# Distance attention: the clamp and the copy of the row minima on VectorE, exponentials over two key tiles

## The reference

```python
q2 = jnp.sum(q * q, axis=-1)
k2 = jnp.sum(k * k, axis=-1)
qk = jnp.einsum('bhid,bhjd->bhij', q, k)
d2 = jnp.maximum(q2[..., :, None] + k2[..., None, :] - 2.0 * qk, 1e-12)
attn = jax.nn.softmax(-jnp.sqrt(d2), axis=-1)
out = jnp.einsum('bhij,bhjd->bhid', attn, v)
...
x = x + (out @ wo.T + bo) * g
```

## Time and profile before

| what | value |
|---|---|
| median of 3 runs | 3808.49 us |
| the profiled execution: its own time | 3799.39 us |
| its span | 3797.3 us |
| mean granted TensorE clock over the span | 0.907 |
| the distance stage in it, from the first minimum to the end | about 3099 to 3797 us |
| mean length of a group's step, from 3432 to 3684 us (12 steps) | 21.0 us |
| busy in these 252 us: ACT, POOL, DVE, PE | 240.5, 231.0, 217.5, 196.0 us |

### The profile page before, as it was taken

How to read it: one execution, slowest core, us unless ns; L and a number is a source line. 1 busy time by engine, 2 the same in 40 slices (tenths; PEclk the granted TensorE clock), 3 DMA queues, 4 the chain that set the end, 5 groups by cost and what they waited for, 6 DMA issues and landing times. The chain is left out here.

```text
span 3797.3 us, 55242 instructions
## 1 busy us (share of the span) xinstructions
PE 3184.6 (84%) x16225; PEld 1672.8 (44%) x16225; DVE 3031.4 (80%) x4845; ACT 2297.1 (60%) x2738; POOL 1814.5 (48%) x904
## 2 busy tenths in 40 slices
PE   7767888888997997877889999899987777877776
PEld 3322333332335886655523334499975531111111
DVE  6878999999995776865678988577757768888887
ACT  4776666667772334643446666522226549999998
POOL 0008998999993111011200000034436538999996
PEclk9878999999998998987879999999998877888888
DMA  4543333323322345955742334144444733344432
GB/s 127 200 175 121 144 146 145 145 96 145 124 69 74 110 152 162 207 139 187 248 136 73 77 72 95 48 101 89 88 78 159 204 105 105 115 127 120 129 117 84
DMA packets 313743, 478.18 MB, mean 126 GB/s; under 512 B 50839, under 2 KB 256280, under 8 KB 293134
## 3 DMA queue, kind: packets, MB, share of 16 engines
q1 hardware_dynamic: 256894, 408.82, 33.8%
q10 hardware_dynamic: 44432, 51.10, 5.0%
q0 software_dynamic: 12288, 16.79, 2.7%
HBM read 322.48 MB, written 153.91 MB: 125 GB/s over the span
## 5 line engine op out<-in xcount | busy, mean ns | idle before, releaser
L1225 PE MATMUL mamba_psum<-mamba_hc,scan_ident 128*128 128x512 f32 x1024 | 548.7, 643 | 90.1 <-DVE mamba_hc L1133 72.1
L3643 POOL TENSOR_TENSOR distance_dist<-distance_dist,distance_least_all 128x2048 f32<-128x2048 f32 x124 | 559.0, 4540 | 74.9 <-DMA distance_least_all<-distance_least_rows 74.8
L1156 DVE TENSOR_TENSOR_SCAN mamba_psum<-mamba_psum,mamba_drive 128x512 f32<-128x512 f32 x352 | 414.9, 1216 | 22.9 <-issue 10.5
L2784 DVE TENSOR_REDUCE causal_row_max<-causal_psum 128x1 f32<-128x512 f32 x512 | 333.0, 683 | 78.0 <-PE causal_psum L2854 68.0
L1225 PEld LDWEIGHTS mamba_psum<-mamba_hc,scan_ident 128*128 128x128 f32 x1024 | 175.8, 195 | 418.0 <-DVE mamba_hc L1133 254.9
L2743 ACT ACTIVATE causal_probs<-causal_psum 128x1024 f32<-128x1024 f32 x256 | 250.6, 1021 | 122.0 <-PE causal_psum L2877 121.8
L3819 PE MATMUL distance_psum<-distance_shared_k_stacks,distance_shared_q_stacks 102*128 102x512 bf16 x512 | 208.7, 504 | 116.9 <-DVE distance_least L3737 56.5
L3737 DVE TENSOR_REDUCE distance_least<-distance_psum 128x2 f32<-128x1024 f32 x256 | 294.2, 1213 | 8.3 <-PE distance_psum L3819 8.0
L3773 DVE TENSOR_SCALAR distance_dist<-distance_psum 128x1024 f32<-128x1024 f32 x192 | 227.0, 1219 | 80.5 <-PE distance_psum L3834 80.5
L1076 POOL TENSOR_TENSOR mamba_drive<-late_channels,scan_b_all 128x1024 f32<-128x1024 f32 x64 | 149.9, 2355 | 289.3 <-POOLq L32 289.3
L1120 ACT ACTIVATE mamba_psum<-mamba_dt,scan_a_neg 128x512 f32<-128x512 f32 x256 | 167.3, 683 | 140.8 <-DVE mamba_hc L1133 140.3
(11 more groups left out here) (473 smaller groups left out, 8593.3 us busy)
## 6 DMA issues: line engine op xcount, KB each, us to landing
distance_least_all<-distance_least_rows SPq DMA_DIRECT2D x32, 1024.0 KB, 4.7
scan_b_all<-bc SPq DMA_DIRECT2D x16, 1024.0 KB, 4.6
scan_c_all<-bc SPq DMA_DIRECT2D x16, 1024.0 KB, 6.6
mamba_b_all<-bc SPq DMA_DIRECT2D x16, 1024.0 KB, 5.1
mamba_c_all<-bc SPq DMA_DIRECT2D x16, 1024.0 KB, 7.1
choice_w<-L_ffn_w SPq DMA_DIRECT2D x16, 1024.0 KB, 5.4
z<-mamba_in_z SPq DMA_DIRECT2D x8, 1024.0 KB, 3.9
xc<-mamba_in_xc SPq DMA_DIRECT2D x8, 1024.0 KB, 3.9
```

The source lines that it names most:

```text
L1156: dve.tensor_tensor_scan(out, bank, drive[:, n % DRIVES], 0.0, ALU.mult, ALU.add).then_inc(h_ready, 1)
L1225: pe.matmul(ps[:, Y_BANK + m % 2], ident[:, :], hc[:, n % PRODUCTS], start=False, stop=(s == DS - 1)).then_inc(y_summed, 1)
L2784: dve.reduce_max(row_max[:, g % 2, u:u + 1], ps[:, u % 2], AX.X).then_inc(a_max, 1)
L3643: pool.tensor_tensor(dist[:, g % 2, kt], dist[:, g % 2, kt], least_all[:, g % 2], ALU.subtract).then_inc(shifted, 1)
```

## The change

```diff
@@ -3558,6 +3558,7 @@
         UNITS = GH * TT // 2
         ACT_UNITS = 2
         DVE_UNITS = UNITS - ACT_UNITS
+        LEAST_UNIT = 3
         BUFFERS = 3
         LAST = (NB - 1, NG - 1)
         K_LOADS = 2 * (len(STACK) + 1)
@@ -3690,13 +3691,9 @@
 
                         act.wait_ge(pv_done, n * TT + 1)
                         floor_scores(0)
-                        act.wait_ge(a_min, n * UNITS + UNITS + 1)
-                        act.activation(least[:, g % 2], least[:, g % 2], ACT.Relu, bias=minus_floor[:, 0:1]).then_inc(least_clamped, 1)
                         act.wait_ge(least_clamped, n + 1)
-                        act.activation(least[:, g % 2], least[:, g % 2], ACT.Sqrt, bias=floor[:, 0:1]).then_inc(least_ready, 1)
+                        act.activation(least[:, g % 2], least[:, g % 2], ACT.Sqrt).then_inc(least_ready, 1)
                         floor_scores(1)
-                        act.wait_ge(least_turned, n + 3)
-                        act.copy(least_t[:, g % 2], ps[0:GH * TT, 7, 0:P]).then_inc(least_copied, 1)
                         for kt in range(TT):
                             if kt == 0:
                                 act.wait_ge(above_floor, (n + 1) * ACT_UNITS)
@@ -3706,14 +3703,17 @@
                                 act.activation(dist[:, g % 2, kt], dist[:, g % 2, kt], ACT.Sqrt).then_inc(sqrt_ready, 1)
                     if out is not None:
                         b, g = out
-                        for kt in range(TT):
-                            if is_last(out):
-                                act.wait_ge(last_shifted, kt + 1)
-                            else:
-                                act.wait_ge(shifted, (b * NG + g) * TT + kt + 1 + 2 * TT)
-                            act.activation(dist[:, g % 2, kt], dist[:, g % 2, kt], ACT.Exp, scale=-1.0).then_inc(p_ready, 1)
-                            if is_last(out) and kt == 0:
-                                load_gx(NB - 1)
+                        for kt in range(0, TT, 2):
+                            pieces = [slice(kt, kt + 1), slice(kt + 1, kt + 2)] if is_last(out) else [slice(kt, kt + 2)]
+                            for piece in pieces:
+                                if is_last(out):
+                                    act.wait_ge(last_shifted, piece.stop)
+                                else:
+                                    act.wait_ge(shifted, (b * NG + g) * TT + piece.stop + 2 * TT)
+                                act.activation(dist[:, g % 2, piece], dist[:, g % 2, piece], ACT.Exp,
+                                               scale=-1.0).then_inc(p_ready, piece.stop - piece.start)
+                                if is_last(out) and piece.stop == 1:
+                                    load_gx(NB - 1)
 
                 act.wait_ge(floor_set, 2)
                 run(act, step)
@@ -3736,6 +3736,14 @@
                             dve.wait_ge(least_turned, n + 1)
                         dve.tensor_reduce(least[:, g % 2, h * TT + 2 * j:h * TT + 2 * j + 2], ps[:, pair(UNITS + u)], op=ALU.min,
                                           axis=AX.X).then_inc(a_min, 1)
+
+                def clamp_least(b, g):
+                    dve.wait_ge(a_min, (b * NG + g) * UNITS + UNITS + 1)
+                    dve.tensor_scalar(least[:, g % 2], least[:, g % 2], D2_MIN, None, ALU.max).then_inc(least_clamped, 1)
+
+                def copy_least(b, g):
+                    dve.wait_ge(least_turned, b * NG + g + 3)
+                    dve.tensor_copy(least_t[:, g % 2], ps[0:GH * TT, 7, 0:P]).then_inc(least_copied, 1)
 
                 def shift_last():
                     b, g = LAST
@@ -3773,6 +3781,8 @@
                             dve.tensor_scalar(dist[:, g % 2, kt, j * 2 * T:(j + 1) * 2 * T],
                                               ps[:, pair(u)].rearrange("p h t -> p (h t)"), D2_MIN, None,
                                               ALU.max).then_inc(clamped, 1)
+                            if u == LEAST_UNIT:
+                                copy_least(*mid)
                     if proj is not None and not isinstance(proj, int):
                         add_bias(proj, 0)
                     if before is not None:
@@ -3793,8 +3803,11 @@
                     elif proj is not None:
                         finish_last(0)
                         finish_last(1)
+                    if first is not None:
+                        clamp_least(*first)
 
                 minima(0, 0)
+                clamp_least(0, 0)
                 dve.wait_ge(bo_loaded, DMA)
                 run(dve, step)
 
@@ -3874,7 +3887,7 @@
                     for u in range(UNITS):
                         if mid is not None:
                             second_scores(*mid, u)
-                            if u == 3:
+                            if u == LEAST_UNIT:
                                 turn_least(*mid)
                         if before is not None and u in (2, 3):
                             output(*before, u)
```

## The result

The changed kernel takes 3874.23 us (median of 4 runs, 3869.74 to 3884.91), the kernel before 3809.21 us beside it (4 runs, 3807.86 to 3812.81): a ratio of 1.0173 [1.0149, 1.0198], 1.7% slower. The profiled execution of after is the longest of its four, 3884.91 us; that of before, 3799.39 us, lies 9.8 us under its median of 3809.21. First, the windows over the distance stage of each kernel, from the first floor_scores(0) to the last, 31 steps. Columns as in the earlier trace rows; first the kernel before, then after.

The account below looks back on a forecast made before the run. No engine is full; a chain of waits through ACT's queue from floor_scores(0) to the transpose sets the step. 3799.39 + 48.1 (29 x 1.66) - 1 = 3846.5 us profiled, 3855.5 us median; range 3830 to 3892.

Parts of the forecast that it names:

- The clamp leaves ACT: On ACT: table load 0.18 us earlier and square root without bias 0.10 us shorter, 0.28 us less per round.
- The clamp is held by POOL: On DVE: the SBUF-to-SBUF clamp waits until POOL's running subtraction ends, taking 2 to 4 us instead of 0.2.
- The rival that it is not held: On DVE: the clamp runs unhindered and only ACT's shorter part works, -9.3 us, 3799.2 us; chance 12%.
- How long: Clamp on DVE: held to the end of POOL's third subtraction, 2.95 us behind floor_scores(0) in the mean.
- the step behind the projection work: One step in four, POOL's block not started by the load: third subtraction's end taken at 3.4 us behind floor_scores(0).
- DVE does not get in between: Rival: the clamp waits for POOL's whole block, 4.5 us more a step, 130 us more, 3986 us; chance 3%.
- The table load stands behind the clamp's wait: On ACT: load starts 3.08 us after floor_scores(0), not 1.32; step 1.66 us longer, 29 steps, 48.1 us.
- The clock falls in the new gap: Rival on PE: product behind the transpose falls to the low clock in every step, 26 us added, 3882; chance 13%.
- Copy and exponentials at nothing: Copy on DVE, 0.3 us, hidden; exponentials over two tiles on ACT hidden, up to 3 us left in the range.

Follow-up runs that it names:

- e7: Kernel before with only the clamp moved to DVE, written as a tensor_reduce; copy on ACT and four exponentials as before: 3786.39 us, ratio 0.9962.
- e1: Changed kernel with the clamp as a tensor_reduce (maximum over pairs of minimum and floor) at the same place on DVE: 3794.34 us, ratio 0.9966 to the kernel before.
- e3: Kernel before with only the clamp moved to DVE as a tensor_scalar, square root without bias: 3859.06 us, ratio 1.0146.
- e2: Changed kernel with clamp and square root's bias back on ACT; copy on DVE and paired exponentials kept: 3806.82 us, ratio 1.0001 to the kernel before.
- e4: Changed kernel, but each POOL subtraction waits until the one before has reported its end: 3834.46 us, ratio 1.0071 to the kernel before.
- e6: Changed kernel, but POOL waits for its last projection addition to end before the next block of subtractions: 3832.88 us, ratio 1.0088 to the kernel before.
- e5: Changed kernel with each POOL subtraction cut in two of 128x1024, eight in a block: 3855.96 us, ratio 1.0151 to the kernel before.

## Why the prediction was right, and where its sum was not

The direction, the cause and the range held: 3874.23 us lies in 3830 to 3892, and the loss was forecast as 47 us and came as 65. Step by step:

- *The clamp leaves ACT, 0.28 us per round.* Right: the table load comes 1.13 us behind floor_scores(0), not 1.32, and in e7 the transpose follows 0.29 us sooner in the mean. e7 shows its price by itself: 14 us by its ratio (0.38% of 3802; 9 to 19 by the interval) against the 9.3 worked out. The rest may be the clock, 0.86 for 0.83; that is argued, not shown.
- *The clamp is held by POOL.* Right. e1 shows it from the one side (never held as a reduction, ratio 0.9966) and e3 from the other (1.0146 by the clamp alone). The rival that it is not held fell; its time, 3799, is near what e1 and e7 came to, 3796 and 3794 by their ratios. The Trainium skill (Advanced Engine Details and Errata, section "VectorE Performance Modes") lists no fast mode for tensor_reduce; that the reduction was never held agrees with it. One row was misread for this step: the four clamps out of PSUM from 3467.69 on the earlier trace rows are not in the middle of POOL's block, which ends at 3469.58. The reading holds by the clamp of unit 2 at 3463.73, 1.23 us in the middle of that block, and in after 65 such clamps that lie wholly inside one of POOL's instructions take 1.20 to 1.23 us each.
- *How long: to the end of the third subtraction, 2.95 us behind floor_scores(0).* Right for the blocks that a landing starts, in which all clamps but one (the first, after two) end after 3.00 subtractions. Wrong for the step behind the projection work, taken at 3.4 us behind floor_scores(0): there the hold goes to the end of the block, 3493.33 - 3483.75 = 9.6 us behind it. That is the rival "DVE does not get in between", given 3%, in a quarter of the steps instead of in all. The 7.99 us for four instructions beside POOL, on which it was put so low, have POOL in single instructions that stand 0.08 us apart; the earlier trace rows show the blocks with a pause and those without it, and the prediction took the two for alike in this. By the rule that it had cited from the Trainium skill (SBUF — State Buffer, section "SBUF: two separate sides") the second comer waits for one whole instruction. The 24 other clamps agree with it; the 7 long ones wait for more than one, and the measurement decides. The same section says that deep queues would have to be drained for sharing; whether that is why a wait on POOL helps, no run here shows.
- *The table load stands behind the clamp's wait, +1.66 us a step, 29 times.* Wrong. The load starts 1.13 us behind floor_scores(0) whether the clamp is held or not. In the 24 steps without a long hold the square root starts only 0.4 us later in the mean. Such a step is 20.2 / 24 = 0.8 us longer, half of the 1.66, and that mostly in the five with 3.5 to 4.1 us of hold (23.5 to 24.2 us against 21.0).
- *The clock falls in the new gap.* Given 13% as a case by itself, for all steps. It came in the 7 long steps, with 0.65 to 0.76 granted and the product at 1.94 us in each, and in four others with holds of 3.6 to 4.1 us, where the product took 1.32 to 1.94 us. A long step costs 7.9 us in the mean (55.4 / 7) for a hold of 8.7: the square root starts 6.0 us later, since the load was hidden, the product takes 0.9 us longer, and the last 1.0 us lies behind it and was not followed.
- *Copy and exponentials at nothing.* Right: e2, 1.0001 [0.9992, 1.001]. The copy took 0.27 us against 0.3 estimated.

So two errors stood against each other. The sum had 29 steps of 1.66 us; in the profiled run there are 24 of 0.8 (+20) and 7 of 7.9 (+55), 75 us in a pair of profiles whose medians differ by 65. That the range held is in part luck: without the long holds (e4, e6) the time is 3834 and 3833 us, at the lower end of the range, and the long holds, which the forecast did not have, brought it up to 3874. e4 and e6, which take the long holds away by two different means, leave 0.7% and 0.9% of the 1.7%; e5, which makes the short ones shorter and the long ones longer, leaves 1.5%.

What stays open: why POOL's instructions without a pause keep DVE out to the last of them, while a pause before the first or between two lets it in at the next end; and what in the form of the instruction decides. Beside the reduction, DVE's transpose from SBUF to SBUF (L430, 128x512) was not held either: one starts at 3483.36, inside POOL's block, and takes 0.70 us like the others of its line, and the clamps of 128x1024 out of PSUM are not held. A tensor_scalar of 128x16 out of or into PSUM in the same place was not tried.

## What to carry to other kernels

Before a small SBUF-to-SBUF tensor_scalar is put on VectorE beside a busy GpSimd, look for its shape in another stage and read its maximum, not its median; then ask how GpSimd's instructions stand, and not only how long each is. If the work must be there, write it as a reduction, or leave a wait between GpSimd's instructions: e7 and e1 gained 0.4 and 0.3% by the first, and e4 got back more than half of the loss by the second. And before a wait is priced, ask what the waiting engine can do ahead of it: here a table load of 1.28 us ran during the hold.

## What was not expected of the hardware

- A 128x16 clamp is held to the end of the whole run of POOL's instructions (8.1 to 9.3 us with four of 4.51, 10.45 to 10.95 with eight of 2.3 behind the projection work) if the run began without a pause, and to the end of the running one after a pause as short as 0.23 us before it (e6) or 0.08 us between (e4). Two clamps in a run of eight without a pause between its fours, told under e6, got in all the same.
- In the profile a held instruction is a busy one. Nothing of the 75 us appears as DVE's waiting; it appears as 9.34 us of a TENSOR_SCALAR over 16 elements, and as ACT's idle time behind it.
- The table load of an activation starts ahead of the semaphore wait of that activation: 3484.89, while the clamp it waits for ended at 3493.33.
